# Third tile's first-layer product ahead of the first convolution, on TensorE, in the ramp of a fused two-layer kernel

## The chip, the cores and the metric

The kernel runs on one core of a Trainium2 chip. The metric is the device time of one execution in microseconds (us). The engines are TensorE (PE), VectorE (DVE), ScalarE (ACT), GpSimd (POOL) and SyncE (SP, which here only issues DMAs). Each engine works through its own list of instructions in order; semaphores (`wait_ge`, `then_inc`) tie the lists together.

## The reference

The input x is 64 samples of 64 channels by 1024, in float32. Two layers are added to it, each a small channel mixing followed by a 1024 by 1024 product:

```python
# layer 0: channel mixing with weights that depend on the sample, then an fp8 product
out = jnp.einsum('boi,bih->boh', agg_w, x) + agg_b[:, :, None]
fp8_x, x_inv_scale = quantize_tensorwise(xm)          # one scale for the whole tensor
fp8_wt, w_inv_scale = quantize_tensorwise(weight.T)
x = x + (fp8_x @ fp8_wt) * (x_inv_scale * w_inv_scale) + bias
# layer 1: grouped 9-tap convolution along the 1024 axis, then a product with dequantised int4 weights
out = lax.conv_general_dilated(x, weight, (1,), [(4, 4)], feature_group_count=4, ...) + ctx + bias
x = x + out @ W.T + bias1
```

Since layer 0 has one quantisation scale for the whole mixed tensor, every tile must be mixed before the first one can be quantised.

## The kernel before

Two samples make one tile of 128 rows by 1024 columns; there are T = 32 tiles. All 32 mixed tiles stay on chip in `Y`.

**First phase** (0 to about 95 us): PE mixes the tiles while the weights of both products are prepared and turned on PE into `f0T` and `f1T`. It ends with the maximum over everything, from which the scale follows.

**Second phase**: every tile t passes through this chain. (1) DVE and ACT quantise it (`first_widen`, `first_quantise` for tiles 0 to 2; `scaled`, `offset`, `quantise` from tile 3). (2) The quantised tile is turned into `qT`: for tiles 0 to 2 by transposes on PE (`turned_first_q`, line 1107) and copies on ACT (`keep_first_q`, line 626), from tile 3 by a DMA transpose (line 388). (3) PE's first-layer product, 16 matmuls of 128x512 into the banks `ps[0]` and `ps[1]` (`first_ffn0`, line 1120, for tiles 0 to 2; `ffn0`, line 1130, afterwards). (4) DVE adds the residual and frees those banks (`residual0`, line 900). (5) The sum is split into a high half, on ACT (`hi`, line 641), and a low half, on DVE (`lo`, line 910). (6) The split rows are moved between partitions: tiles 0 and 1 by eight DMAs each, half issued by SP (`move`, line 412) and half by POOL (line 530); from tile 2 through DRAM by two DMAs (lines 395 and 399). (7) PE's convolution, 48 matmuls of 128x128 into `ps[4]` and `ps[5]`, one bank for each of the tile's two samples b (`conv`, line 1146). (8) The result is split again, on ACT (`yhi`, line 646) and DVE (`ylo`, line 917), bank by bank. (9) PE's second-layer product, two halves of 16 matmuls into `ps[2]` and `ps[3]`, which DVE has filled with the fixed part before (`seed`, line 929; `ffn1`, line 1156). (10) DVE adds it to the tile (`residual1`, line 923) and SP stores it.

The order of the work is written out by hand for every engine. In the steady state PE's step for tile t is: `ffn0(t)`, `ffn1(t - 2)` half 0, `conv(t - 1)`, `ffn1(t - 2)` half 1. The ramp before it is spelled out; its last part is what the change touches. What PE waits for there:

- `first_ffn0(2, 0, 16)` waits for both halves of `qT` of tile 2 (`qT_in[0]` at 24 and 32, from ACT) and for `x1_done` at 3 and 4, that is for DVE's `residual0(1)`, which frees `ps[0]` and `ps[1]`. It gives `f0_done` 5 and 6.
- `conv(0, True)` waits for the DMAs of tile 0 for each sample (`moved_sp[b]`, `moved_pool[b]`). It gives `conv_done` 1 and 2.
- `ffn1(0, ...)`, the first thing in `step(2, ...)`, waits for `ylo_done` at 2, that is for the second bank of `conv(0)` to have gone through ACT and DVE, and for the seeds.

Others in the ramp: ACT's list is `keep_first_q(2, 0)`, `keep_first_q(2, 1)`, `hi(1)`, `yhi(0)`, `scaled(3)`, `scaled(4)`, `hi(2)`, `yhi(1)`. DVE's is `residual0(1)`, the seeds of tile 0, `lo(1)`, `ylo(0)`, `residual0(2)`, `offset(3)`, `quantise(3)`, `lo(2)`, `residual1(0)`, `ylo(1)`, `seed(1)`. SP's is the moves of tile 0, the reload of x for tile 2, the moves of tile 1 (those of sample b also wait for `conv_done` at b + 1), the reload and the DMA transpose of tile 3, and the two DMAs of tile 2's split rows.

Of the kernel before, what the change touches and what calls it, by code (L numbers as in the profile page):

```python
# [5 lines left out]
def adaln_ffn_kernel(nc, x, cond, fside, cw0, cb0, cw1, cb1, cw2, cb2, cwk, cbk,  # L6
# [44 lines left out]
    with ctx:  # L51
# [936 lines left out]
        def _(pe):  # L988
# [108 lines left out]
            def turned_first_q(t, h):  # L1097

                pb = ps[(6 if t == 2 else 4) + h][:, 0:H // 2].bitcast(bf16)
                pe.wait_ge(first_q, 2 * t + h + 1)  # L1100
                if t == 1:
                    pe.wait_ge(qT_in[0], 8 * h + 8)
                if t == 2:
                    pe.wait_ge(fixed_ev, 2 * h + 2)
                for k in range(4):
                    at = (4 * h + k) * P
                    last = nc.tensor.transpose(pb[:, k * P:(k + 1) * P], qn[t % 2][:, at:at + P], ident_b)
                last.then_inc(q_turned, 1)

            def first_ffn0(t, n, before):  # L1110
                for kh in range(2):
                    pe.wait_ge(qT_in[n], before + 8 * kh + 8)
                    for h in range(2):
                        if kh == 0:
                            if t:
                                pe.wait_ge(x1_done, 2 * t - 1 + h)
                            else:
                                pe.wait_ge(shifted_ev, h + 1)
                        for k in range(4 * kh, 4 * kh + 4):
                            last = mm(ps[h][:, :], qT[n][:, k, :], f0T[:, k, h * H:(h + 1) * H],  # L1120
                                      start=(k == 0), stop=(k == KT - 1))
                        if kh:
                            last.then_inc(f0_done, 1)
# [10 lines left out]
            def conv(t, first=False):  # L1134
                if not (isinstance(t, int) and t < 2):
                    pe.wait_ge(split_in, 16 * t - 16)
                for b in range(NB):
                    if isinstance(t, int) and t < 2:
                        pe.wait_ge(moved_sp[b], 32 * t + 32)
                        pe.wait_ge(moved_pool[b], 32 * t + 32)  # L1140
                    if not first:
                        pe.wait_ge(ylo_done, 2 * t - 1 + b)
                    for g in range(G):
                        parts = [(xp, wp, h) for xp, wp in ((0, 0), (0, 1), (1, 0)) for h in range(2)]
                        for j, (xp, wp, h) in enumerate(parts):
                            last = mm(ps[4 + b][:, g * P:(g + 1) * P], convin[:, b * G + g, h:h + S, xp],  # L1146
                                      taps16[:, wp, h, g].rearrange("p r a -> p (r a)"),
                                      start=(j == 0), stop=(j == len(parts) - 1))
                    last.then_inc(conv_done, 1)
# [54 lines left out]
            wsum_part(1)  # L1204
            turned_first_q(2, 0)
            turned_first_q(2, 1)
            pe.wait_ge(taps_split, 4)
            conv(0, True)
            first_ffn0(2, 0, 16)

            def step(t, n, ge, first=False):
                if not first:
# [38 lines left out]
```

## Time and profile before

| | us |
|---|---|
| three runs | 531.87, 533.1, 532.83 |
| their median | 532.83 |
| profiled execution, its own time | 533.22 |
| profiled execution, span from first to last instruction | 531.3 |
| PE busy | 509.3 (96%) |
| DVE busy | 410.6 (77%) |
| ACT busy | 245.5 (46%) |
| POOL busy | 60.4 (11%) |

The span is that of the instructions; the execution's own time is 1.92 us longer. Matmuls overlap in the record (each is shown longer than its distance from the next), so in a run of matmuls the start of the next piece of work tells more than the busy time. "Granted clock" (PEclk) is the share of TensorE's full 2.4 GHz that the chip gave: 1.00 or, at 1.2 GHz, 0.50.

### The profile page before, as it was taken

Reading aid. Unit: us, or ns where it says so; the run is one execution under the profiler, and the core shown is the slowest. Engines: PE = TensorE matmul, PEld = TensorE weight load, DVE = VectorE, ACT = ScalarE, POOL = GpSimd, SP = SyncE. Lnnn points to the kernel's source line nnn. Section 1 sums busy time; section 2 is a strip of 40 time slices with the busy share of each in tenths; the row PEclk is TensorE's granted clock in tenths of the full one; section 3 lists DMA queues with packets and bytes.
Section 4 is the critical chain, followed back from the end, with each engine's and each line's share of the span. In section 5 each row is a group of like instructions: output and inputs, shape, how many; then the busy total and the mean of one; then the engine's idle time right before and its main releaser. Section 6 shows DMA issues by size and latency. Waiting matters only on the chain.

```text
span 531.3 us, 9515 instructions
## 1 busy us (share of the span) xinstructions
PE 509.3 (96%) x3495; PEld 286.1 (54%) x3526; DVE 410.6 (77%) x519; ACT 245.5 (46%) x287; POOL 60.4 (11%) x67
## 2 busy tenths in 40 slices
PE   4999999879999999999999999999999999999997
PEld 3644444345555555555555555555555555555563
DVE  4789999885887777777777777777777777777652
ACT  3488897655344444444444444444444444442310
POOL 6257775011000000000000000000000000000000
PEclk9999999979999999999999999999999999999999
DMA  6999491144665566666666656566565656566632
GB/s 185 399 394 400 159 350 66 47 114 101 202 199 179 179 180 182 181 183 185 185 186 185 183 179 179 179 179 179 179 179 179 179 179 182 179 187 186 200 121 79
DMA packets 85387, 100.22 MB, mean 189 GB/s; under 512 B 34348, under 2 KB 66862, under 8 KB 85374
## 3 DMA queue, kind: packets, MB, share of 16 engines
q1 hardware_dynamic: 84554, 99.29, 59.4%
q0 software_dynamic: 448, 0.55, 0.6%
q10 hardware_dynamic: 372, 0.20, 0.1%
q8 instruction: 8, 0.13, 0.1%
q14 instruction: 5, 0.04, 0.0%
HBM read 58.41 MB, written 32.75 MB: 172 GB/s over the span
## 4 chain that ended last, share of the span: by engine, by line
PE 82%; DVE 11%; issue 2%; POOL 2%; ACT 1%; DMA 1%; SPq 0%; POOLq 0%; DVEq 0%; ACTq 0%
PE pair L1156 42%; PE pair L1130 19%; PE pair L1146 17%; DVE stat L802 5%; PE pair L1038 2%; PE pair L1120 1%; DVE work L729 1%; PE pair L1026 1%; DVE work L817 1%; DMA work<-work 1%; POOL work L454 1%; DVE Y L817 1%; DVE work L732 1%; POOL fixed L487 1%; POOL Y L467 1%
## 5 line engine op out<-in xcount | busy, mean ns | idle before, releaser
L1156 PE MATMUL pair<-f1T,work 128*128 128x512 f16 x1024 | 231.0, 379 | 0.0
L1156 PEld LDWEIGHTS pair<-f1T,work 128*128 128x128 f16 x1024 | 98.9, 98 | 113.5
L608 ACT ACTIVATE work<-Y,consts 128x1024 bf16 (+1 forms) x29 | 33.3, 1148 | 186.7 <-DVE work L891 186.7
L910 DVE TENSOR_TENSOR work<-Y,work 128x512 f16<-128x512 f16 (+1 forms) x64 | 71.2, 1118 | 46.6 <-ACT work L641 45.6
L1130 PE MATMUL pair<-f0T,work 128*128 128x512 bf16 x435 | 98.6, 379 | 1.5
L1146 PEld LDWEIGHTS pair<-taps,work 128*128 128x128 f16 x1536 | 90.7, 99 | 9.8 <-issue 2.4
L1146 PE MATMUL pair<-taps,work 128*128 128x128 f16 x1536 | 93.4, 222 | 2.3 <-DMA work<-work 2.3
L923 DVE TENSOR_TENSOR Y<-pair,Y 128x512 f32 (+1 forms) x64 | 43.9, 687 | 44.2 <-PE pair L1156 44.2
L641 ACT CAST work<-Y 128x512 f16 (+1 forms) x64 | 69.5, 1135 | 17.9 <-DVE Y L900 15.6
L1130 PEld LDWEIGHTS pair<-f0T,work 128*128 128x128 bf16 x464 | 45.4, 98 | 54.8
L1038 PE MATMUL pair<-Y,work 128*128 128x512 f32 x128 | 61.8, 618 | 1.1 <-ACT Y L581 0.7
L646 ACT CAST work<-pair 128x512 f16<-128x512 f32 x64 | 37.2, 584 | 35.3 <-PE pair L1146 33.9
L929 DVE SCALAR_TENSOR_TENSOR pair<-work,consts,fixed 128x512 f32<-128x512 f32 x64 | 48.0, 752 | 0.1
L900 DVE SCALAR_TENSOR_TENSOR Y<-pair,stat,Y 128x512 f32 (+1 forms) x64 | 45.1, 743 | 2.6 <-PE pair L1120 1.4
L917 DVE TENSOR_TENSOR work<-pair,work 128x512 f16<-128x512 f32 x64 | 41.3, 682 | 3.9 <-ACT work L646 3.8
L581 ACT ACTIVATE Y<-pair,consts 128x1024 f32<-128x1024 f32 (+1 forms) x33 | 35.9, 1090 | 10.1 <-PE pair L1038 10.0
L884 DVE SCALAR_TENSOR_TENSOR Y<-work,Y 128x1024 bf16 (+1 forms) x29 | 35.5, 1225 | 4.0
L802 DVE TENSOR_REDUCE stat<-Y 128x1 f32<-128x1024 f32 (+2 forms) x23 | 36.5, 1629 | 2.0 <-ACT Y L581 1.9
L891 DVE SCALAR_TENSOR_TENSOR work<-work,Y 128x1024 bf16<-128x1024 bf16 x29 | 35.5, 1225 | 1.2
L1038 PEld LDWEIGHTS pair<-Y,work 128*128 128x128 f32 x128 | 23.1, 196 | 24.8 <-issue 23.7
L609 ACT ACTIVATE Y<-Y,stat (+1 forms) x29 | 32.9, 1134 | 0.0
L487 POOL TENSOR_TENSOR fixed<-Y,work 128x1024 bf16<-128x1024 f32 x8 | 24.1, 3006 | 19.9 <-DVE Y L734 19.9
(150 smaller groups left out, 234.8 us busy)
## 6 DMA issues: line engine op xcount, KB each, us to landing
Y<-in_x_dram SPq DMA_DIRECT2D x64, 512.0 KB, 3.9
out_dram<-Y SPq DMA_DIRECT2D x31, 512.0 KB, 3.8
split_rows<-work SPq DMA_DIRECT2D x30, 520.0 KB, 2.6
work<-split_rows SPq DMA_DIRECT2D x30, 520.0 KB, 3.9
Y<-in_L_ffn_weight_dram SPq DMA_DIRECT2D x8, 512.0 KB, 6.5
Y<-in_L_ffn_W_q_dram SPq DMA_DIRECT2D x5, 512.0 KB, 14.6
work<-in_L_ffn_W_q_dram SPq DMA_DIRECT2D x3, 512.0 KB, 15.2
work<-work SPq DMA_DIRECT2D x8, 65.0 KB, 3.6
```

The source lines that it names most:

```text
L641: nc.scalar.copy(split[:, r, h:h + S, 0], v[:, r, :]).then_inc(hi_done, 1)
L646: nc.scalar.copy(y1s[n][:, 0, :, b * C:(b + 1) * C].rearrange("p r (g a) -> p g r a", g=G), ps[4 + b][:, :].rearrange("p (g r a) -> p g r ...
L802: nc.vector.tensor_reduce(stat[:, n:n + 1], part, AX.X, ALU.max, apply_absolute_value=True).then_inc(mixed_red, 1)
L900: nc.vector.scalar_tensor_tensor(out=v, in0=ps[h][:, :], scalar=acc_neg, in1=v, op0=ALU.mult, op1=ALU.add).then_inc(x1_done, 1)
L910: nc.vector.tensor_tensor(split[:, r, s, 1], v[:, r, :], split[:, r, s, 0], ALU.subtract)\
L917: nc.vector.tensor_tensor(part(1), ps[4 + b][:, :].rearrange("p (g r a) -> p g r a", g=G, r=R8), part(0), ALU.subtract).then_inc(ylo_done, 1)
L923: nc.vector.tensor_tensor(v, ps[2 + h][:, :], v, ALU.add).then_inc(res_done, 1)
L929: nc.vector.scalar_tensor_tensor(out=ps[2 + h][:, :], in0=wsum[:, c], scalar=ctxcol[:, bass.ds(t, 1)], in1=fixed[:, c], op0=ALU.mult, op1= ...
L1038: last = mm(ps[2 * (t % 2) + h][:, :], mixw[:, t, :], slot(t)[:, h * H:(h + 1) * H], start=True, stop=True)
L1130: last = mm(ps[h][:, :], qT[n][:, k, :], f0T[:, k, h * H:(h + 1) * H], start=(k == 0), stop=(k == KT - 1))
L1146: last = mm(ps[4 + b][:, g * P:(g + 1) * P], convin[:, b * G + g, h:h + S, xp], taps16[:, wp, h, g].rearrange("p r a -> p (r a)"), start=( ...
L1156: last = mm(ps[2 + h][:, :], y1s[n][:, e, k, :], f1T[:, k, h * H:(h + 1) * H], start=False, stop=(e == 1 and k == KT - 1), skip_group_chec ...
```

## The change

In PE's list the product of tile 2 goes ahead of the convolution of tile 0. No other engine's list is changed, no instruction is added or removed, and each keeps its own waits; the wait for the convolution's taps moves with the convolution.

```diff
             wsum_part(1)
             turned_first_q(2, 0)
             turned_first_q(2, 1)
+            first_ffn0(2, 0, 16)
             pe.wait_ge(taps_split, 4)
             conv(0, True)
-            first_ffn0(2, 0, 16)
 
             def step(t, n, ge, first=False):
                 if not first:
```

## Rows read from the trace of the kernel before

**Rows 1.** The page: the chain that ended last, its shares by engine.

```profile
PE 82%; DVE 11%; issue 2%; POOL 2%; ACT 1%; DMA 1%; SPq 0%; POOLq 0%; DVEq 0%; ACTq 0%
```

**Rows 2.** That chain in order of time, in the loop: start, us, what.

```profile
146.61 3.40 PE pair L1130 x15
...
153.46 2.68 PE pair L1146 x48
...
159.65 3.40 PE pair L1130 x15
```

**Rows 3.** Timeline of PE in the ramp: start, us, what [idle before <-releaser].

```profile
112.52 0.40 PE L1107 MATMUL pair<-small,work 128*128 128x128 bf16 x4 [1.00 <-DVE work L875]
115.20 5.27 PE L1146 MATMUL pair<-taps,work 128*128 128x128 f16 x48 [2.29 <-DMA work<-work]
120.53 3.40 PE L1120 MATMUL pair<-f0T,work 128*128 128x512 bf16 x15
123.76 3.62 PE L1156 MATMUL pair<-f1T,work 128*128 128x512 f16 x16
127.22 2.84 PE L1146 MATMUL pair<-taps,work 128*128 128x128 f16 x48
...
133.57 3.40 PE L1130 MATMUL pair<-f0T,work 128*128 128x512 bf16 x15
...
140.26 2.84 PE L1146 MATMUL pair<-taps,work 128*128 128x128 f16 x48
```

**Rows 4.** Timeline of DVE in the ramp.

```profile
112.38 1.40 DVE L900 SCALAR_TENSOR_TENSOR Y<-pair,stat,Y 128x512 f32<-128x512 f32 x2
...
121.13 0.69 DVE L917 TENSOR_TENSOR work<-pair,work 128x512 f16<-128x512 f32 x1 [1.32 <-ACT work L646]
123.17 1.54 DVE L900 SCALAR_TENSOR_TENSOR Y<-pair,stat,Y 128x512 f32<-128x512 f32 x2 [1.35 <-PE pair L1120]
...
126.42 1.23 DVE L891 SCALAR_TENSOR_TENSOR work<-work,Y 128x1024 bf16<-128x1024 bf16 x1
...
134.75 0.75 DVE L929 SCALAR_TENSOR_TENSOR pair<-work,consts,fixed 128x512 f32<-128x512 f32 x1
```

**Rows 5.** Timeline of ACT in the ramp.

```profile
113.00 0.59 ACT L626 COPY work<-pair 128x512 bf16<-128x512 bf16 x1 [0.77 <-issue]
...
120.51 0.58 ACT L646 CAST work<-pair 128x512 f16<-128x512 f32 x1 [1.94 <-PE pair L1146]
```

**Rows 6.** Timeline of SP, which issues the DMAs.

```profile
119.24 3.38 SPq L412 DMA_DIRECT2D work<-work  x4
...
128.11 1.35 SPq L388 DMA_TRANSPOSE work<-work  x1
...
135.74 0.38 SPq L399 DMA_DIRECT2D work<-split_rows  x1
```

**Rows 7.** SP's second move DMA of tile 1 (119.87 to 120.50), us to landing.

```profile
work<-work SPq DMA_DIRECT2D x1, 65.0 KB, 4.1
```

**Rows 8.** DMAs issued from 127 to 146 us, median us to landing.

```profile
work<-split_rows SPq DMA_DIRECT2D x1, 520.0 KB, 3.9
...
work<-work SPq DMA_TRANSPOSE x2, 4.4
```

**Rows 9.** Stretches of the ramp: length, busy of PE, PEld, DVE, ACT, POOL, then PEclk.

```profile
111.50:113.50 2.00, 0.41 (x5) 0.23 (x4) 1.90 (x4) 1.23 (x3) 0.58 (x2) 1.00 0.67 116
113.50:115.20 1.70, 0.00 (x0) 0.03 (x1) 1.61 (x3) 0.08 (x1) 0.00 (x0) 0.50 0.82 176
115.20:120.30 5.10, 5.10 (x48) 5.10 (x50) 2.73 (x3) 2.65 (x3) 0.79 (x2) 0.50 0.26 92
120.40:123.90 3.50, 3.45 (x17) 1.58 (x17) 1.42 (x2) 2.67 (x3) 1.20 (x3) 1.00 0.82 140
```

**Rows 10.** The mixing's matmuls (line 1038) in stretches near the kernel's start.

```profile
21.33:23.00 1.67, 1.67 (x2) 0.81 (x3) 1.00 1.01 400
...
29.90:31.60 1.70, 1.70 (x5) 0.76 (x4) 1.00 1.00 397
```

## The prediction

> **What bounds the kernel now.** I read the chain that ended last first: PE holds 82% of it [rows 1]. Followed in order of time through the loop, the chain is PE alone: the first-layer product comes back every 159.65 - 146.61 = 13.04 us, and between two of them stand one convolution of 2.68 us and two second-layer halves of 3.45 us, with 0.05 us left over [rows 2]. So nothing else than PE bounds the loop, and a microsecond that PE's list wins before the loop is won at the end, as long as the other engines keep up. Then the timeline of PE just before the loop [rows 3]. It shows two losses at one place. PE stands idle for 1.00 us until 112.52, works 0.40 us, and is idle again for 2.29 us until the first convolution gets its DMAs at 115.20. And that convolution takes 5.27 us, where the next one takes 2.84 us. The stretches with their clock tell why: the granted clock is 1.00 (2.4 GHz) up to 113.5, 0.50 (1.2 GHz) from there to 120.3, and 1.00 again behind it [rows 9]. Last the timelines of DVE, ACT and SP, for what the moved product waits for and who waits for it.
>
> **Part 1: the product moves into the pause.** It needs three things. The first half of tile 2's turned values is copied before the second, which ACT ends at 113.00 + 0.59 = 113.59 [rows 5]; only the last 8 matmuls need that one. The banks: DVE frees them with two instructions in 1.40 us from 112.38 [rows 4], so at 113.08 and 113.78. The 16 matmuls take 3.40 us [rows 3]. With 0.05 us for the signal the first four start at 113.13; the next four want the second bank at 113.98, the last eight the second copy at 114.83, and both are there. At full clock the product ends at 113.13 + 3.40 = 116.53. The convolution's DMAs have been there since 115.20 [rows 3].
>
> **Part 2: the convolution.** It starts at 116.58 and takes 2.68 us [rows 2] at full clock: it ends at 119.26. Before, it ended at 115.20 + 5.27 = 120.47 [rows 3].
>
> **Part 3: a wait is laid bare.** The second-layer product of tile 0 waits for the second bank of the convolution to pass ACT and DVE. Before, this lay beside the moved product: ACT started 0.04 us after the convolution and took 0.58 us (until 121.09) [rows 5], DVE took 0.69 us from 121.13 (until 121.82) [rows 4], while PE was busy until 123.93. Now there is nothing between: 0.04 + 0.58 + 0.04 + 0.69 + 0.05 = 1.40 us of idle PE. ACT and DVE are free for it, as both had been waiting then, for 1.94 and 1.32 us [rows 4, 5]. So the product starts at 119.26 + 1.40 = 120.66 instead of 120.53 + 3.40 = 123.93. That is 3.27 us earlier: 2.07 us of pause are filled (115.20 - 113.13), 5.27 - 2.68 = 2.59 us of slow clock are gone, 1.40 us of new pause are paid; the sum is 3.26, the rest is rounding.
>
> **Part 4: do the others keep up?** Behind the bank's evacuation DVE comes to the residual of tile 2, which started at 123.17 because the moved product ended late [rows 4]. Its product is now long done, so it starts when DVE is free, at 120.61: 2.56 us earlier. DVE's quantising of tile 3, ACT's scaling, the splits of tile 2 and the DMAs behind them follow in that order and move by the same 2.56 us, less than PE's 3.27. What is late next:
> - The convolution of tile 1 would start at 120.66 + 3.45 = 124.11. SP's moves of tile 1 start at 119.24 as before, since they wait for DVE's split, and no longer for the convolution; the second of them, the last that sample 0 needs, lands at 119.87 + 4.1 = 123.97 [rows 6, 7]. Room 0.14 us.
> - Then PE does the second half (until 130.24) and wants tile 3's turned values at 130.29. DVE ends quantising at 126.42 + 1.23 - 2.56 = 125.09 [rows 4], the DMA transpose is issued 0.46 us later (128.11 against 127.65 before) and lands after 4.4 us [rows 6, 8], at 129.95. Room 0.34 us.
> - The seed of tile 1 ends at 134.75 + 0.75 - 2.56 = 132.94 [rows 4]; PE wants it at 133.69. Room 0.75 us.
> - The convolution of tile 2 would start at 137.14. Its rows come by the DMA issued at 135.74 - 2.56 = 133.18, which takes 3.9 us [rows 6, 8]: 137.08. Room 0.06 us. From there PE's step is the longer one, and the room grows.
>
> The last of these could each run over by some tenths, since more of the DMAs now lie close together; they lie behind one another, so the worst of them counts and not the sum. I take nothing for it and keep 0.5 us as its upper bound.
>
> **Part 5: the clock.** The trace of before doesn't show whether the clock still falls. It fell at 113.5, 0.6 us into the long pause, after 0.41 us of PE work in two microseconds [rows 9]. The change adds only 0.37 us of matmuls before that moment; but in place of the 1.7 idle microseconds behind it come dense ones. If the clock does not fall, the term is nothing. If it falls at 113.5, the low stretch should be shorter than the 5.1 us of work that it cost before, for the nearest other row is the start of the mixing: its matmuls came about 0.85 us apart from 21.33 to 24.7 and 0.43 us apart later [rows 10], so the engine worked slowly for some 3.4 us and lost 1.7 us by it. I take the middle of 0 and 1.7, 0.85 us: the three runs of before differ by 1.23 us (531.87 to 533.1) with the same instructions, which is about what a low stretch of changing length at this place would give, and the median of the runs after should lie between the ends too.
>
> The page "TensorE: Matmul & The Clock Gate" of the Trainium skill, section "HAM oscillation — how this bites in real kernels", says that matmul bursts with DMA waits between them start cold each time, and that work put into the waits keeps the clock up. Rows 9 agree on the cold start; by the rule alone the clock term would be 0 and the time 529.95.
>
> **The sum.** The profiled execution took 533.22 us, of which 1.92 us lie outside its span and stay. 533.22 - 3.27 + 0.85 = 530.80. It stands 0.39 us above the median of the runs, but I don't take that off: it paid the full low clock (2.59 us), which is taken out of the sum, and the other runs' lower times would then have less to lose.
>
> **Rivals.**
> 1. *The clock stays low as long as before*, until 120.33. For it: nothing in PE's work before 113.5 changes much. Against: at 113.5 the engine now works instead of idling. PE then does 0.37 us of work at full clock and 6.83 / 2 = 3.41 us of work by 120.33; of 3.40 + 2.68 + 0.05 us 2.35 are left, the convolution ends at 122.68, tile 0's second product starts at 124.08, 0.15 us later than before: 533.37. The new pause eats what the order wins.
> 2. *Slower*: the same, and the new pause of 1.40 us lets the clock fall once more. The change puts two short pauses, each behind short work, in place of one long. The half product behind it (3.45 us) would run at half clock for some 3.4 us and lose 1.7 us: 533.37 + 1.7 = 535.1. It decides from the point where a pause of 1.4 us between dense work is enough. Against it: idle stretches of 1.00 us left the clock at 1.00 in the ramp [rows 3, 9]. The same page, section "A second HAM failure mode: psum-queue depth-cycling", says that frequent small pauses between matmul groups make the clock swing; by it this rival would be the likely one.
> 3. *The chain of DVE, ACT and DMAs takes a part back*: with as little as 0.06 us of room at the convolution of tile 2, a DVE chain that moved forward by 1.0 us instead of 2.56 would make PE wait 1.5 us there, and leave 3.27 - 1.5 = 1.8 us: 531.4. A clock term of up to 1.5 us would hide in the same wait. If that chain did not move at all, its DMA would land at 139.64 and leave 0.7 us: 532.5. For it: three rooms under 0.4 us. Against: every step of the chain that I followed moves with DVE.
>
> That the change doesn't do what it says, because the freed banks come late, is excluded by DVE's row at 112.38, which hangs on nothing moved.
>
> **How the numbers follow.** Forecast (the order pays, the clock term lies between 0 and 1.7, so 529.95 to 531.65): 0.80. Rival 1: 0.08. Rival 2: 0.03. Rival 3: 0.09. The predicted time is 530.8. The range: down to 529.6 (a third of a microsecond below the lowest sum, for a run-to-run difference), up to 532.0, which takes in 0.5 us of the lateness of part 4 on most clock terms and about half of rival 3. A difference under 0.2% of 532.83, 1.07 us, can't be told from none: faster means below 531.76. That holds in nearly all of the forecast and half of rival 3: 0.83; rival 1, the other half of 3 and a rest: 0.14; slower: 0.03.
>
> **What would show it.** The moved product (line 1120) starts at about 113.1, before the convolution, and the idle time of 2.29 us on the DMA is gone. PE idles about 1.4 us, released by DVE's line 917, before tile 0's second-layer product, which starts between 120.7 and 122.4. Line 900 of tile 2 follows line 917 without a gap. The loop still takes 13.04 us per tile. Wrong would be: a granted clock of 0.50 that lasts to 120.3 again, or a second low stretch behind 119; new idle time at lines 1146 or 1130 released by a DMA; or a first loop step that starts earlier than before while the end does not.

## The result, and the profile after

| | before | after |
|---|---|---|
| median of 22 runs each, us | 533.34 (531.87 to 535.33) | 532.0 (530.43 to 534.3) |
| ratio after / before | | 0.9971, 95% interval 0.996 to 0.9981 |
| profiled execution, its own time | 533.22 | 531.97 |
| span | 531.3 | 530.1 |

The change makes the kernel faster by about 0.3%. The median lies at the upper edge of the stated range (529.6 to 532.0), 1.2 us above the predicted 530.8. The new median of before is higher than the 532.83 of the first three runs, so the gain is 1.34 us, where the prediction had 532.83 - 530.8 = 2.03.

Timeline of PE in the kernel after: start, us, what. These rows answer to [rows 3] and to the last of [rows 2].

```profile
112.37 0.40 PE L1107 MATMUL pair<-small,work 128*128 128x128 bf16 x4 [1.00 <-DVE work L875]
113.12 5.30 PE L1120 MATMUL pair<-f0T,work 128*128 128x512 bf16 x16 [0.35 <-DVE Y L900]
118.26 2.84 PE L1146 MATMUL pair<-taps,work 128*128 128x128 f16 x48
122.50 3.63 PE L1156 MATMUL pair<-f1T,work 128*128 128x512 f16 x16 [1.40 <-DVE work L917]
125.97 2.84 PE L1146 MATMUL pair<-taps,work 128*128 128x128 f16 x48
...
132.10 3.62 PE L1130 MATMUL pair<-f0T,work 128*128 128x512 bf16 x16
...
139.01 2.84 PE L1146 MATMUL pair<-taps,work 128*128 128x128 f16 x48
...
145.14 3.62 PE L1130 MATMUL pair<-f0T,work 128*128 128x512 bf16 x16
```

The moved product starts at 113.12, the wait of 2.29 us for the DMAs is gone, and a new one of 1.40 us stands before tile 0's second-layer product, released by DVE's line 917. That product starts at 122.50, against 123.76 before: 1.26 us earlier, and the span is 1.2 us shorter. The convolutions of tiles 1 and 2 (125.97 and 139.01) are both 1.25 us earlier too, and no new wait follows; the loop still takes 145.14 - 132.10 = 13.04 us. The moved product takes 5.30 us instead of 3.40. The stretches tell why (length, busy of PE, PEld, DVE, ACT, POOL, granted clock, DMA share, GB/s), the answer to [rows 9]:

```profile
111.50:113.40 1.90, 0.68 (x6) 0.42 (x7) 1.79 (x4) 1.13 (x3) 0.43 (x1) 1.00 0.71 131
113.50:116.80 3.30, 3.30 (x9) 1.22 (x8) 1.46 (x3) 0.67 (x1) 0.00 (x0) 0.50 0.75 217
117.00:120.00 3.00, 3.00 (x39) 2.29 (x38) 2.14 (x2) 1.48 (x3) 0.00 (x0) 1.00 0.01 3
```

The clock still fell just after 113.4, while the product ran, and was back before 117.0: 3.4 us at 0.50, where the profiled execution of before had 6.8 us.

DVE goes straight from the bank's low half to tile 2's residual, without the gap of 1.35 us that it had there [rows 4]:

```profile
121.75 0.69 DVE L917 TENSOR_TENSOR work<-pair,work 128x512 f16<-128x512 f32 x1 [0.65 <-ACT work L646]
122.36 1.40 DVE L900 SCALAR_TENSOR_TENSOR Y<-pair,stat,Y 128x512 f32<-128x512 f32 x2
```

Each run comes with its mean granted clock, and this sorts most of the times. In a span of some 531 us one stretch of 3.4 us at 0.50 gives a mean of 0.997, and 6.8 us give 0.994; 0.99 is then about 10 us, an estimate from these two, since no execution of that group was profiled. Taken together over the runs of before beside the experiments (88) and the runs of the changed kernel (34):

| mean clock | before: runs, median us (range) | after: runs, median us (range) |
|---|---|---|
| 1.00 | none | 10, 530.59 (530.39 to 531.04) |
| 0.996, 0.997 | 11, 532.8 (531.78 to 533.59) | 16, 532.02 (531.7 to 532.12) |
| 0.993, 0.994 | 36, 533.38 (532.66 to 533.93) | 8, 533.79 (533.5 to 534.3) |
| 0.989, 0.99 | 41, 534.87 (534.39 to 535.62) | none |

The groups of after don't overlap: in this kernel the time follows how long the clock was low. None of the 88 runs of before was without a low stretch. At an equal mean the change is not always a gain: it is 0.8 us faster at 0.996 and 0.997, and 0.4 us slower at 0.993 and 0.994. What it wins is mainly that more runs fall into the higher groups.

### The profile page after: what moved, and what is told of

The parts are those of the page before. It is cut to its first block, busy times and chain, and to the rows that moved or that the text cites. A ratio compares the mean times of both kernels' runs of the same rounds, so it can differ in the third digit from the quotient of the medians.

```text
span 530.1 us, 9546 instructions
## 1 busy us (share of the span) xinstructions
PE 510.3 (96%) x3526; PEld 284.0 (54%) x3526; DVE 410.3 (77%) x519; ACT 245.8 (46%) x287; POOL 60.6 (11%) x67
## 4 chain that ended last, share of the span: by engine, by line
PE 82%; DVE 11%; issue 3%; POOL 2%; ACT 1%; DVEq 0%; POOLq 0%; ACTq 0%
PE pair L1156 42%; PE pair L1130 19%; PE pair L1146 16%; DVE stat L802 5%; PE pair L1038 2%; PE pair L1120 2%; DVE work L729 1%; PE pair L1026 1%; DVE work L817 1%; POOL work L454 1%; DVE Y L817 1%; DVE work L732 1%; POOL fixed L487 1%; POOL Y L467 1%; ACT Y L581 0%
## 5 line engine op out<-in xcount | busy, mean ns | idle before, releaser
L1130 PE MATMUL pair<-f0T,work 128*128 128x512 bf16 x464 | 104.9, 379 | 0.0
L1146 PEld LDWEIGHTS pair<-taps,work 128*128 128x128 f16 x1536 | 88.5, 98 | 7.5
L1146 PE MATMUL pair<-taps,work 128*128 128x128 f16 x1536 | 91.0, 219 | 0.0
```

## The experiments

All ran in 5 rounds beside the kernel before; ratios are to it. Experiments 1 to 4, 5 to 8, 9 to 11, and 12 ran on four different chips, on which the median of before was 534.41, 533.57, 534.59 and 533.63 us; a difference of some tenths between two experiments is only worth reading within one such set. The word "rival" below is that of each experiment's expectation. "Extra matmuls" are 128x512 products of constant weights into a bank whose content nobody reads (line 1183).

**1. The changed kernel again.** No edit.

> The changed kernel again, to see each run's mean granted clock beside its time. Theory: the change's order is worth 3.3 us at full clock, and each run loses to a low-clock stretch that differs by execution. Its runs then fall into groups: mean clock 1.00 at 530.4 to 530.9 us, one stretch of 3.4 us (mean 0.997) at 531.7 to 532.1, and a slowest group (mean 0.994) at 533.5 to 534.3. Rival (the times differ for another reason than the clock): times spread without following the mean clock.

Median 531.99, ratio 0.9962 (0.9942 to 0.9982). Of 12 runs four stood at 1.00 (530.39 to 531.04), five at 0.996 or 0.997 (531.83 to 532.12), three at 0.993 or 0.994 (533.56 to 533.9). The times follow the clock, in the groups that were expected; the rival falls.

**2. The 1.00 us pause filled.**

```diff
             turned_first_q(2, 0)
+            filler(4, 4)
             turned_first_q(2, 1)
```

> Four extra matmuls of 128x512 on PE, into a bank nobody reads, inside the 1.00 us pause before tile 2's second transposes; all else as changed. Theory (the low stretch behind 113.5 comes from PE doing little before it): the clock no longer falls there, the group at 531.7 to 532.1 goes, and most runs are at 530.4 to 530.9. Rival A (the clock falls whatever fills that pause, since the transposes and short products around it are what it answers to): the groups are as in the changed kernel, median 532.0. Rival B (the slowest group comes from the new 1.4 us pause before tile 0's second-layer product): that group stays, at about a fifth of the runs.

Median 531.24, ratio 0.9946 (0.9926 to 0.9966). Five runs at 1.00 (530.13 to 530.48), five at 0.997 (531.99 to 532.56), none below. Its profiled execution was one of the second kind:

```profile
98.00:101.30 3.30, 2.86 (x14) 1.00 (x13) 3.10 (x8) 3.04 (x6) 0.00 (x0) 1.00 0.00 0
101.50:104.70 3.20, 3.20 (x10) 1.15 (x8) 3.13 (x8) 2.79 (x5) 0.00 (x0) 0.52 0.45 164
...
111.00:115.00 4.00, 3.52 (x19) 1.28 (x17) 3.78 (x7) 1.52 (x3) 2.12 (x4) 1.00 0.48 76
```

The clock no longer falls at 113; it falls at 101.6, under tile 0's product, a place where the profiled executions of before, after and experiment 1 show nothing. So there are two places. Rival A falls. Rival B, the new pause, falls too: the slowest group is gone from these ten runs with the new pause left as it is (and stays away in experiments 6 and 9, which leave it too).

**3. The new pause filled as well**: `filler(6, 6)` behind `conv(0, True)`.

> As the run before, and six extra matmuls of 128x512 (1.28 us) in the new pause of 1.40 us behind the first convolution. Theory (that pause alone doesn't lower the clock): as with the front pause filled, within 0.2 us. Rival B (the new pause is what makes the slowest group): the slowest group is gone here and present with the front filled only; median 0.3 to 1 us lower than there.

Median 532.0, ratio 0.9956 (0.9938 to 0.9974). Seven runs at 0.999 or 1.00, five at 0.997, as without it. The new pause isn't what lowers the clock. The median is 0.8 us above that of experiment 2, where I had expected 0.2 at most. Two of the runs at 1.00 took 532.35 and 532.46, five 530.2 to 530.83; what held up those two is open, as none of them was profiled. In the profiled one (530.79) the second-layer product started at 121.24, because DVE's low halves ended only at 121.2: the last of tile 0's DMAs had landed 0.9 us later than in experiment 9, and ACT, DVE and that product with it.

**4. The kernel before, both of its pauses filled.**

```diff
+            filler(4, 4)
             turned_first_q(2, 1)
+            filler(4, 9)
             pe.wait_ge(taps_split, 4)
             conv(0, True)
```

> The kernel before, its order unchanged, with extra matmuls in its two pauses: four in the 1.00 us one and nine (1.9 us) in the 2.29 us one. This takes away the low clock and leaves the pause. Theory: the convolution takes 2.7 instead of 5.3 us, and the kernel gains the 2.6 us of the clock without the change of order: 530.6 us against 533.2. Then of the 3.3 us at full clock most is the clock and only 0.7 us (2.07 filled less 1.40 laid bare) the order. Rival (the convolution is slow because its DMAs still land beside it): it stays at 5.3 us and the time at 533.2.

Median 532.37, ratio 0.9963 (0.9946 to 0.998). Timeline of PE:

```profile
114.40 2.11 PE L1183 MATMUL pair<-f1T 128*128 128x512 f16 x9
116.84 2.84 PE L1146 MATMUL pair<-taps,work 128*128 128x128 f16 x48 [0.34 <-issue]
```

The convolution takes 2.84 us, so its DMAs don't slow it. The five runs at 1.00 took 530.58 to 531.73 (median 531.1, expected 530.6); seven at 0.996 or 0.997 took 532.3 to 533.2, and in the profiled one of them the clock fell at 101.8, ahead of the extra matmuls. In the runs at 1.00 the clock alone, without the order, wins most of the 3.3 us.

**5. The product cut in two around the convolution.**

```diff
-            first_ffn0(2, 0, 16)
+            first_ffn0(2, 0, 16, [0])      # the first 8 matmuls
             pe.wait_ge(taps_split, 4)
             conv(0, True)
+            first_ffn0(2, 0, 16, [1])      # the last 8
```

> The changed kernel with tile 2's product cut in two: its first 8 matmuls before the first convolution, its last 8 behind it, where they cover the way of the convolution's second bank through ACT and DVE. Theory: the 1.40 us pause goes, but tile 0's second-layer product can't start earlier than DVE has that bank (lo of tile 1, then ylo of tile 0, about 120.5 to 121.2), so at full clock it gains only 0 to 0.3 us on the changed kernel: fullest-clock runs at 530.2 to 530.8, pause under 1 us. Rival (the pause laid bare is a full 1.4 us loss): fullest-clock runs at 529.2 to 529.6.

Median 531.53 (6 runs), ratio 0.995 (0.9932 to 0.9969); one run at 1.00, 530.54, as the theory has it. It stands on that one run; experiment 12 repeats it. The profiled one was of mean clock 0.994 and shows low stretches at both places in one execution, from 101.3 and from 115.0:

```profile
101.50:104.70 3.20, 2.98 (x7) 1.03 (x7) 3.13 (x8) 2.79 (x5) 0.00 (x0) 0.50 0.48 164
104.90:108.00 3.10, 3.10 (x19) 1.41 (x16) 2.09 (x4) 1.06 (x3) 0.00 (x0) 1.00 0.51 169
...
115.10:118.30 3.20, 3.20 (x10) 1.27 (x10) 1.54 (x3) 0.92 (x2) 0.00 (x0) 0.50 0.78 220
```

The three runs at 0.994 took 531.91 to 532.11, some 1.5 us more than the run at 1.00, where the changed kernel lost 3.2 us at that mean. So what a low stretch costs depends on the order too. In the profiled one PE goes from the last 8 matmuls straight into the second-layer product, without the wait that experiment 12 shows there at full clock; that this accounts for the difference isn't shown.

**6. Everything filled**: experiment 2, and `filler(5, 4)` in the 0.96 us pause at 94.2, `filler(5, 2)` in the 0.44 us pause before tile 0's first transposes.

> As with the front pause filled, and six extra matmuls earlier: four in the 0.96 us pause in which DVE finds the maximum of the mixed tensor (94.2 to 95.1) and two in the 0.44 us pause before tile 0's first transposes. Theory (in half of the executions the clock falls already at 101.4, behind that stretch of pauses and short products, and costs 1.7 to 2 us, in the kernel before as well): no run has a low stretch; all at 530.1 to 530.9, median 530.4. Rival (that earlier fall has another cause): two groups stay, at 530.3 and at 532.2.

A miss, and a useful one. Median 532.11, ratio 0.997 (0.9956 to 0.9984): 11 of 12 runs at 0.999 or 1.00, and still none under 531.81. The theory was right on the clock and wrong on the time: something else took 1.7 us. DVE's timeline (first row) and PE's (second) show it:

```profile
106.58 1.41 DVE L900 SCALAR_TENSOR_TENSOR Y<-pair,stat,Y 128x512 f32<-128x512 f32 x2 [1.65 <-DMA Y<-in_x_dram]
```

```profile
107.47 3.61 PE L1120 MATMUL pair<-f0T,work 128*128 128x512 bf16 x16 [1.00 <-DVE Y L900]
```

Tile 0's reload of x, 3.0 to 3.3 us in the profiled executions of experiments 1 to 5, took 5.4.

**7. The kernel before, only its 1.00 us pause filled.** The four extra matmuls of experiment 4, without the nine.

> The kernel before with the four extra matmuls in its 1.00 us pause only; the 2.29 us pause for the first convolution's DMAs stays. Theory (the long pause suffices by itself to lower the clock in most executions): no run at mean clock 1.00, or few; the convolution still takes 4 to 5.3 us in the profile, and the median is 1 us or more above that of the kernel before with both pauses filled (532.37), near 533. Rival (the 1.00 us pause was the cause, and the long one alone does nothing): median 532.4, as with both filled.

The second miss. Median 531.79, ratio 0.9964 (0.9947 to 0.9982); six of 12 runs at 1.00 (530.38 to 531.2). Timeline of PE, and the stretches:

```profile
115.37 2.84 PE L1146 MATMUL pair<-taps,work 128*128 128x128 f16 x48 [2.23 <-DMA work<-work]
```

```profile
111.50:113.50 2.00, 1.51 (x12) 0.61 (x10) 1.90 (x4) 1.23 (x3) 0.81 (x2) 1.00 0.67 111
113.50:115.30 1.80, 0.00 (x0) 0.00 (x0) 1.80 (x3) 0.32 (x1) 0.00 (x0) 1.00 0.80 190
115.40:118.00 2.60, 2.60 (x48) 2.60 (x49) 0.12 (x1) 1.30 (x2) 0.00 (x0) 1.00 0.41 159
```

PE waits 2.23 us and the clock stays at 1.00. In these six runs the long pause alone lowers nothing, while none of the 88 runs of before, which differ only in the four matmuls, was at 1.00: what comes before the long pause has its part. Of the other six, four stood at 0.997 and two at 0.993 (534.03 and 534.21); where the clock fell in those isn't recorded. Four matmuls that compute nothing win about as much as the change (0.9964 here, 0.9962 in experiment 1).

**8. Everything filled and the product cut**: 5 and 6 together.

> The split product with the ten extra matmuls of the fully filled kernel: the best that I can put together. Theory: no low stretch and no pause behind the convolution; all runs at 530.0 to 530.7, the same as fully filled within 0.3 us, since DVE and the DMAs of tiles 0 and 1 set the time there. Rival (PE's pause was the bound): 529.2 to 529.6.

Median 532.35, ratio 0.9969 (0.9958 to 0.9981): the reload took 5.3 us here too. As in 6, the clock's gain is given back.

**9. Only two of the six early matmuls**: experiment 2 and `filler(5, 2)`.

> Front pause filled (four extra matmuls), and of the six earlier ones only the two in the 0.44 us pause before tile 0's first transposes; product whole and ahead of the convolution. Theory 1 (the fetch of PE's instructions, one DMA of 16 KB, came at 103.3 instead of 108 us in the two fully filled kernels, inside the reload of tile 0's x, which then took 5.3 us instead of 3.1): with fewer instructions added ahead, the reload is back at 3.1 us. Theory 2 (two matmuls there keep the clock up at 101.4): no run below mean clock 1.00; then the median is 530.4. If only theory 1 holds: two groups, 530.3 and 532.2. If neither: 532.

Median 530.57, ratio 0.9932 (0.9917 to 0.9947), all five runs at 1.00 and within 530.43 to 530.82. Both theories hold, and the reload took 3.3 us. Timeline of PE:

```profile
113.27 3.61 PE L1120 MATMUL pair<-f0T,work 128*128 128x512 bf16 x16 [0.35 <-DVE Y L900]
116.72 2.84 PE L1146 MATMUL pair<-taps,work 128*128 128x128 f16 x48
120.97 3.63 PE L1156 MATMUL pair<-f1T,work 128*128 128x512 f16 x16 [1.40 <-DVE work L917]
124.43 2.84 PE L1146 MATMUL pair<-taps,work 128*128 128x128 f16 x48
```

This is the prediction's parts 1 to 4 at full clock.

**10. Six small matmuls early**: the changed kernel with six matmuls of 64 columns in the 0.96 us pause, nothing else.

> The changed kernel with nothing but six small extra matmuls (64 columns, 0.3 us in all) in the 0.96 us pause at 94.2: as many instructions as the six larger ones of the fully filled kernel had, with little work in them. Theory (the place of the instruction fetch delays the reload): fetch near 103, reload 5.3 us, DVE's residual of tile 0 waits for it up to 1.7 us; no run under 531.5, median 532.3 to 533. Rival (the reload was slow for another reason, such as the chip or the larger matmuls): reload 3.1 us and the same groups as the changed kernel, median 532.0 with runs at 530.4.

Median 533.75, ratio 0.999 (0.9978 to 1.0002), lowest 532.92. Some 0.3 us of extra work in a pause takes back the change's whole gain. The median is above the 532.3 to 533 that I expected, for the clock was low too: none of the 11 runs stood at 1.00, and six at 0.993 or 0.994. DMA queues and issues of this kernel in 102 to 103 and 101 to 102 us, then DVE's timeline:

```profile
q8 instruction: 1, 0.02, 9.2%
```

```profile
Y<-in_x_dram SPq DMA_DIRECT2D x1, 512.0 KB, 5.3
```

```profile
106.26 1.41 DVE L900 SCALAR_TENSOR_TENSOR Y<-pair,stat,Y 128x512 f32<-128x512 f32 x2 [1.53 <-DMA Y<-in_x_dram]
```

The stretches of that execution:

```profile
113.40:116.70 3.30, 2.66 (x9) 1.07 (x10) 3.09 (x5) 0.74 (x2) 0.06 (x1) 0.50 0.73 162
116.80:119.90 3.10, 3.10 (x9) 1.11 (x8) 1.54 (x2) 2.15 (x2) 0.00 (x0) 0.50 0.33 128
```

The clock was low for 6.8 us, from 113.3 to 120.0, where that of the changed kernel was low for 3.4. So of the 2.56 us that it is slower than the profiled execution of after (534.53 against 531.97) only a part is the reload's; experiment 6, with the clock up, has the reload's share alone, 1.7 us.

The same two rows of experiment 9, whose packet comes between 108 and 109:

```profile
q8 instruction: 1, 0.02, 5.9%
```

```profile
Y<-in_x_dram SPq DMA_DIRECT2D x1, 512.0 KB, 3.3
```

**11. The order of before with the pauses of experiment 9 filled**, and the nine matmuls in its long pause.

> The kernel before, its order unchanged, with its 0.44 us, 1.00 us and 2.29 us pauses filled (two, four and nine extra matmuls): beside the first run of this set it leaves only the order as a difference, with the clock up in both. Theory: slower than that one by 0.7 us (2.07 us filled less 1.40 us laid bare), 531.1 against 530.4. Rival (the order is worth nothing once the clock is up): equal within 0.2 us.

Median 530.9 (530.71 to 533.13, 6 runs), ratio 0.9943 (0.9925 to 0.9962), the clock up in all. Timeline of PE (the view ends at 128, so that the last row is not whole):

```profile
115.17 2.84 PE L1146 MATMUL pair<-taps,work 128*128 128x128 f16 x48 [0.33 <-issue]
117.84 3.62 PE L1120 MATMUL pair<-f0T,work 128*128 128x512 bf16 x16
121.30 3.62 PE L1156 MATMUL pair<-f1T,work 128*128 128x512 f16 x16
125.74 2.46 PE L1146 MATMUL pair<-taps,work 128*128 128x128 f16 x41 [0.83 <-DMA work<-work]
```

Against experiment 9 the second-layer product starts 121.30 - 120.97 = 0.33 us later, and the medians differ by 0.33 us. The order by itself is worth a third of a microsecond, half of what I had reckoned; with intervals of 0.3% each this rests on the timelines more than on the medians. The wait of 0.83 us for tile 1's DMAs in this execution (531.77) shows how near they are: the last that it waited for took 5.71 us to land. Why another run, at 1.00 as well, took 533.13 isn't known.

**12. The split product on the kernel of experiment 9.**

> The fastest kernel so far (two extra matmuls in the 0.44 us pause, four in the 1.00 us one, product ahead of the convolution; 530.57 us) with the product cut in two around the convolution. Theory: the 1.40 us pause behind the convolution was only in part PE's to win, for DVE has the bank's low half no earlier than 120.5 (lo of tile 1, then ylo of tile 0) and tile 1's DMAs land near 124: gain 0 to 0.4 us, runs at 530.1 to 530.8, mean clock 1.00. Rival (PE's pause is the bound): gain 1.0 to 1.4 us, 529.2 to 529.6.

Median 530.45 (530.08 to 530.68), ratio 0.9938 (0.9924 to 0.9951). Timeline of PE, then DVE's:

```profile
118.30 1.67 PE L1120 MATMUL pair<-f0T,work 128*128 128x512 bf16 x7
120.72 3.63 PE L1156 MATMUL pair<-f1T,work 128*128 128x512 f16 x16 [0.75 <-DVE work L917]
```

```profile
117.33 2.14 DVE L910 TENSOR_TENSOR work<-Y,work 128x512 f16<-128x512 f32 x2 [1.97 <-ACT work L641]
119.38 1.28 DVE L917 TENSOR_TENSOR work<-pair,work 128x512 f16<-128x512 f32 x2
```

PE's pause is halved, and the product still starts only when DVE has made the low halves, since DVE's split of tile 1 ends at 119.4 and comes first in its list. The product starts 0.25 us earlier than in experiment 9, but the convolution behind it does not (124.41 against 124.43). The chain that ended last, from 112 to 132, says why: start, us, what.

```profile
112.40 3.57 DMA work<-work
...
116.15 1.16 ACT work L641
...
117.33 2.15 DVE work L910 x2
...
120.13 4.23 DMA work<-work
...
124.41 2.86 PE pair L1146 x48
```

It runs through the DMAs of tile 0, the split of tile 1 and the DMAs of tile 1, and holds nothing of PE before 124.41; in experiment 9 the same view has PE's product and convolution in it, and no DMA. The pause laid bare was thus hardly PE's to win: behind it the DMAs of tile 1 come next. Experiments 9 and 12 are the fastest kernels here, and can't be told from each other.

## Why the prediction was right or wrong

*The range held by luck.* The forecast proper ended at 531.65, the order's gain with the largest clock term. The median of 532.0 lies beyond that and inside the range only through what the range allowed for late DMAs, and those did not come: what was larger than supposed was the clock term.

*The order (parts 1 to 3): right as a mechanism, 0.48 us too large.* At full clock the prediction wanted the product at 113.13, the convolution at 116.58, the second-layer product at 120.66. Experiment 9 has 113.27, 116.72 and 120.97. Its gain in the timeline is 123.76 - 120.97 = 2.79 us, and 533.22 - 2.79 = 530.43 is exactly the time of that execution. The sum had 3.27: 0.17 us too much because I took the start of before as 120.53 + 3.40 = 123.93, though [rows 3] have it at 123.76; 0.14 us because the product itself started that much later; and 0.17 us because from the convolution's start to the next product it took 2.84 + 1.40 us and not 2.68 + 1.40: I had taken the convolution's share of a dense chain, though the wait behind it begins only at its recorded end. The 1.40 us of part 3 were met to the hundredth. For the same reason the product of the kernel after, at 122.50, lies just outside the 120.7 to 122.4 that I had given for it.

*The others keep up (part 4): right.* In experiment 9 the convolution of tile 1 follows without a wait of PE, and the changed kernel shows no new idle time behind it. Rival 3 did not occur in it. But the smallest room was where I had put 0.14 us, at tile 1's DMAs: experiment 11's 0.83 us show that it is a matter of the execution, and experiment 12 runs at that limit.

*The clock (part 5): right that it may fall, mis-sized as a term.* I took 0.85 us, the middle of 0 and 1.7. Measured from the group at 1.00 the median loses 532.0 - 530.59 = 1.4 us. Only 10 of 34 runs were free of a low stretch; 16 lost 1.43 us, within my ends; and 8, with a mean of 0.993 or 0.994, lost 3.2 us (533.79 - 530.59), beyond both of my ends. Two things can make such a run, and the record doesn't tell them apart, as none of the 8 was profiled. The clock can fall at two places in one execution, at 101.3 and at 115.0, as experiment 5 shows, whose list is the same up to there. Or it can stay low for 6.8 us at the second place, as in before and in experiment 10, which is rival 1. In experiment 2 the group is gone with the second place, and either would give that. I had read low stretches from one profiled execution, which had only one place. The three runs at hand gave a spread of 1.2 us, and 22 give 3.5.

The end of 1.7 us was met (PE's product took 5.30 us instead of 3.62), but the rows that I took it from don't carry it: [rows 10] have the granted clock at 1.00 in both stretches, so they don't show that the slow mixing matmuls there come from the clock. That the low stretches under the products then were of 3.4 us is luck as far as the record goes.

*Why the change pays at all.* I ascribed 2.59 us to the clock and 0.7 to the order. That the clock has the larger part holds; the order was worth half of that, 0.33 us at full clock (experiments 9 and 11). The rest of the 1.34 us is put down to a clock that is low for a shorter time, 3.4 us against 6.8 in the profiled executions, by subtraction and by the shift between the groups of the table. But the cause isn't the long pause as such: experiment 7 keeps it and has the clock up in half of its runs. Against rival 2 the prediction took the pause of 1.00 us for harmless, since the clock was still at 1.00 behind it; experiments 2 and 7, which fill only that pause, show that it has its part in the fall that follows. Why the same list falls in some executions and not in others stays open.

*The rivals.* Rival 1 (low as long as before, 533.4) did not occur in the profiled execution; experiment 10's had 6.8 us at 0.50 with the changed order (mean 0.994), so it can, and up to 8 of the 34 runs may be it. Rival 2, the slower side, is refuted by the result, and its mechanism by experiments 2 and 3. The clock stayed at 1.00 behind the new pause of 1.40 us in experiment 9. "TensorE: Matmul & The Clock Gate" of the Trainium skill, section "A second HAM failure mode: psum-queue depth-cycling", says that frequent small pauses between groups of matmuls make the clock swing; this one pause did not. The clock fell 0.3 us into the product that now fills the wait. By the same page's section "HAM oscillation — how this bites in real kernels", as the prediction read it, work in the wait keeps the clock up and the time would have been 529.95; the trace doesn't agree for 24 of 34 runs, and the 10 at 1.00 gave 530.59.

## What to carry to other kernels

In this ramp of short products and waits the clock of the next dense stretch differed from one execution to the next, and so did where it fell. In such a case take the mean granted clock of many runs, sort the times by it, and only then compare orders of work. A few matmuls without a purpose in the pauses were worth more here than the better order (experiments 7 and 11), but added instructions also moved the fetch of the instruction list, and where it landed beside an urgent load, up to 1.7 us went again (experiment 6). When a wait is laid bare behind a moved step, follow the chain that ended last once the wait is covered: covering part of PE's pause of 1.4 us won nothing that can be told from noise (530.45 against 530.57), since the DMAs of tile 1 came next.

## What the runs showed of the hardware that I had not expected

- **An instruction fetch beside a load.** In the eleven profiled executions whose fetch on queue q8 came near 108 us, tile 0's reload of 512 KB took 3.0 to 3.4 us. In the three where it came between 102 and 104 us, inside the reload (experiments 6, 8, 10), it took 5.3 to 5.4 us. In experiment 10 nothing but six small matmuls had been added. Eleven against three executions show the coincidence, and experiment 10 was expected to give it before it ran; why one packet of 0.02 MB costs 2.1 us isn't shown.
- **The clock can fall under work.** In the kernel after, PE idled 1.00 us and 0.35 us and had been at its dense product for 0.3 us when the granted clock went from 1.00 to 0.50; in experiment 7 it idled 2.23 us in one piece and the clock stayed up. The length of the longest pause alone didn't tell here.
- **The low stretches** were of 3.4 us each in the profiled executions of after and of experiments 1, 2, 4 and 5, and of 6.8 us in that of before and of experiment 10.
